# Four small transformer layers in one kernel: MLP up projections as three fp32r passes, pairwise statistics, new step orders

## What is computed

```
L0: x = x + attn(ln1(x), ctx) Wo + b;            x = x + gelu(ln2(x) W1 + b1) W2 + b2     16 heads of 16
L1: a = attn(x, [ctx, x]) Wo + b + x;            x = x + gelu(rms(a) W1 + b1) W2 + b2     16 heads of 16
L2: x = x + attn(ln(x), ctx) Wo + b  (twice);    x = x + gelu(ln(x) W1 + b1) W2 + b2      16 heads of 128, plus a bias key and value
L3: x = x + attn(ln1(x), ln1(x)) Wo + b;  x = x + attn(ln2(x), ctx) Wo + b;  x = x + gelu(ln3(x) W1 + b1) W2 + b2
```

## Time and profile before

| | |
|---|---|
| median of 3 runs | 1079.56 us (1079.14 to 1081.27) |
| profiled execution | 1081.11 us, its span 1079.8 us |
| PE busy | 1045.6 us, 97% |
| DVE, ACT, POOL busy | 706.6, 602.2, 572.0 us |
| granted TensorE clock | 0.998 of 2.4 GHz |
| stages | A to about 305 us, B to about 814 us, C to the end |

### The profile page before, as it was taken

The page is one execution under the profiler, slowest core; times in us unless marked ns, Lnnn a source line. Parts: engine busy times, 40 slices in busy tenths (PEclk is TensorE's granted clock), DMA queues, the critical chain, the costliest instruction groups (busy, mean ns, idle before and its releaser), DMA issues.

```text
span 1079.8 us, 20226 instructions
## 1 busy us (share of the span) xinstructions
PE 1045.6 (97%) x7794; PEld 917.4 (85%) x7794; DVE 706.6 (65%) x1088; ACT 602.2 (56%) x1323; POOL 572.0 (53%) x618
## 2 busy tenths in 40 slices
PE   6899999999999999999999999999999999988999
PEld 5788788788888999999998999999998887866887
DVE  6888778879537556555658655655654377988840
ACT  4998887778653232223334323322226489999972
POOL 7555535455664434333466434443525378999860
PEclk9999999999999999999999999999999999999999
DMA  9200000000113222122120111101100000000000
GB/s 336 112 2 21 2 1 1 2 1 2 49 42 96 70 69 59 40 79 79 40 76 26 40 40 39 40 29 31 31 1 2 1 1 1 2 2 2 10 11 20
DMA packets 33783, 40.66 MB, mean 38 GB/s; under 512 B 2111, under 2 KB 31257, under 8 KB 32025
## 3 DMA queue, kind: packets, MB, share of 16 engines
q1 hardware_dynamic: 33689, 39.38, 11.1%
HBM read 38.32 MB, written 1.05 MB: 36 GB/s over the span
## 4 chain that ended last, share of the span: by engine, by line
PE 77%; POOL 9%; issue 5%; DVE 5%; ACT 4%; DMA 0%; SPq 0%; POOLq 0%; DVEq 0%; ACTq 0%
PE psum L489 14%; PE psum L663 13%; PE psum L557 10%; PE psum L677 7%; PE psum L723 7%; PE psum L583 5%; PE psum L711 5%; PE psum L691 4%; POOL C tile L1371 3%; PE psum L573 3%; PE psum L598 3%; PE psum L700 2%; PE psum L541 2%; PE psum L610 2%; POOL C tile L1377 2%
## 5 line engine op out<-in xcount | busy, mean ns | idle before, releaser
L1459 POOL TENSOR_TENSOR B tile<-B tile,B rec 128x1024 f32<-128x1024 f32 x32 | 60.7, 1897 | 207.8 <-DVE B rec L994 207.8
L1377 POOL TENSOR_TENSOR A tile<-A tile,outer rec 128x1024 f32<-128x1024 f32 x48 | 90.4, 1894 | 99.4 <-DVE outer rec L887 99.4
L1257 ACT ACTIVATE B own<-B max 128x8 f32<-128x8 f32 x32 | 6.7, 210 | 163.1 <-DVE B tile L981 163.1
L1198 ACT ACTIVATE A tile<-A tile,outer min 128x128 f32<-128x128 f32 (+1 forms) x256 | 92.1, 459 | 3.6 <-DVE outer min L880 3.5
L1126 ACT ACTIVATE B kT<-psum,B bcol 128x1024 f32<-128x1024 f32 x32 | 35.6, 1113 | 90.8 <-PE psum L663 90.8
L489 PE MATMUL psum<-A hT,weights 128*128 128x256 f32 x352 | 81.2, 381 | 2.0 <-ACT A hT L1126 2.0
L489 PE MATMUL psum<-C hT,weights 128*128 128x256 f32 x352 | 80.3, 381 | 1.3 <-DVE C tile L870 1.1
L1198 ACT ACTIVATE C tile<-C tile,outer min 128x128 f32<-128x128 f32 x256 | 77.5, 398 | 3.2 <-DVE outer min L880 3.2
L1022 DVE TENSOR_TENSOR x_all<-x_all,psum 128x512 f32<-128x512 f32 x64 | 42.6, 685 | 54.3 <-PE psum L723 54.3
L489 PEld LDWEIGHTS psum<-A hT,weights 128*128 128x128 f32 x352 | 65.2, 190 | 12.5 <-ACT A hT L1126 3.2
L489 PEld LDWEIGHTS psum<-C hT,weights 128*128 128x128 f32 x352 | 65.5, 190 | 11.3 <-issue 2.1
(11 more groups left out here) (197 smaller groups left out, 3113.6 us busy)
## 6 DMA issues: line engine op xcount, KB each, us to landing
weights<-in_weights_c SPq DMA_DIRECT2D x6, 1024.0 KB, 6.9
raw<-in_wq SPq DMA_DIRECT2D x32, 128.0 KB, 2.7
raw<-in_wk SPq DMA_DIRECT2D x32, 128.0 KB, 2.8
raw<-in_wv SPq DMA_DIRECT2D x16, 256.0 KB, 2.7
raw<-in_wo SPq DMA_DIRECT2D x16, 256.0 KB, 2.8
weights<-in_weights_a SPq DMA_DIRECT2D x1, 3072.0 KB, 21.7
weights<-in_weights_a SPq DMA_DIRECT2D x1, 2048.0 KB, 11.3
wide<-in_bias_v SPq DMA_DIRECT2D x2, 1024.0 KB, 10.6
```

The lines of the kernel that those rows point to most:

```text
L1198: i = act.activation(of_head, of_head, ACT.Exp, bias=part.min[:, u % 4, h:h + 1], scale=-1.0)
L1377: pool.tensor_tensor(tile(u, ly.nk), tile(u, ly.nk), part.rec[:, u % 4, 0:ly.per].unsqueeze(2).to_broadcast([P, ly.per, ly.nk]), ALU.mult) ...
L1459: pool.tensor_tensor(tv, tv, m.brec[:, h, :].unsqueeze(2).to_broadcast([P, B, S]), ALU.mult).then_inc(s["normalised"].sem, s["normalised"] ...
```

## The change

What it does:

- **Up projections in three passes.** `up` multiplies as stage B does, 12 fp32r matmuls a step. For this each MLP's up weights are cut by GpSimd in four quarters (`cut_up`, steps `cut L0 0` and so on; for M2 in turns 2 to 4 and 7 of the second round of stage B), and each stream's features into `hi` and `lo`: for L0, M2 and L3c VectorE drains the transposed rows with scale and offset into the space of `xn` (`split`), ScalarE rounds that into `hi` (`upper`), GpSimd subtracts (`lower`). For L1, whose norm has no offset, ScalarE drains straight into `hi` and VectorE subtracts it from the bank.
- **Space.** `lo` of the weights takes the place of the weights, `hi` that of `raw` (L0), of L0's first weights (L1), of used rows of biases and a tile of stage C (M2), and of new tiles (L3c). Stage C has four key and value slots in place of five. The int32 mask has a tile of its own.
- **Statistics** of both batches of a stream in one step: two `bn_stats`, two `bn_aggr`, one addition and one power on 128x2; `xn` is one step a stream too.
- **Loads.** SyncE loads heads 0 and 1 of stage B, which go to `raw`, behind L0's last `up`.
- **Orders.** Both texts are new; they have 413 and 302 steps in place of 437 and 330. Units of L3 run as s0, s1, s2, c0, c1, s3, c2, c3.

The diff, cut to its core:

```diff
-SLOTS = {"L0": (0, 1, 0, 1), "L1": (0, 1, 0, 1), "L3s": (0, 1, 2, 3), "L3c": (NS, 0, 1, 2)}
+SLOTS = {"L0": (0, 1, 0, 1), "L1": (0, 1, 0, 1), "L3s": (0, 1, 2, 0), "L3c": (3, 1, 2, 3)}
...
+        self.w_hi = {"L0": quarters(self.raw_hi), "L1": quarters(self.weights_lo), "M2": [self.rows_hi[:, n * C:(n + 1) * C, :] for n in range(3)] + [m2_hi],
+                     "L3c": l3_hi}
...
-                features(event, part.xn[k], z, "ACT")
+                features(event, part.xn[k], z, "parts" if of == "mlp" else "ACT")
...
         def up(name, k, o, z):
+            event, lo = (name, "up", k, o), lo_signal(name)
             if o == 0:
-                wait_features((name, "mlp", k))
-            if name == "L0":
-                once("w_mlp0_loaded", 16)
-            by_features((name, "up", k, o), "up_projected", "up_drained", m.w[UP[name][0]], part.hT[k], o, z)
+                pe.wait_ge(s[lo].sem, s[lo].at((name, "mlp", k)))
+            pe.wait_ge(s["up_lo_made"].sem, s["up_lo_made"].at((name, o // 2)))
+            claim(z, "up_drained", event)
+            d.take(event, z)
+            w = m.w_hi[name][o // 2], m.w_lo[UP[name][0]][:, :, o * P:(o + 2) * P]
+            h = part.hi[k], part.lo[k]
+            for n in range(2):
+                for c in range(C):
+                    for wp, hp in PASSES:
+                        i = pe.matmul(bank(z)[:, n * T:(n + 1) * T], w[wp][:, c, n * P:(n + 1) * P], h[hp][:, c, :],
+                                      start=(c, wp, hp) == (0, 0, 0), stop=c == C - 1 and wp == 1)
+            i.then_inc(s["up_projected"].sem, s["up_projected"].mark(event))
...
+        def split(name, k):
+
+            event, (scale, offset) = (name, "mlp", k), LN[name, "mlp"]
+            z, scale = d.bank[event], m.col[scale]
+            if offset is None:
+                dve.wait_ge(s["hi_drained"].sem, s["hi_drained"].at(event))
+                for c in range(C):
+                    i = dve.scalar_tensor_tensor(out=part.lo[k][:, c, :], in0=bank(z)[:, c * T:(c + 1) * T], scalar=scale[:, c:c + 1],
+                                                 in1=part.hi[k][:, c, :], op0=ALU.mult, op1=ALU.subtract)
+                i.then_inc(s["lo_drained"].sem, s["lo_drained"].mark(event))
+                return
+            dve.wait_ge(s["turned"].sem, s["turned"].at(event))
+            for c in range(C):
+                i = affine(part.h(k)[:, c, :], bank(z)[:, c * T:(c + 1) * T], scale[:, c:c + 1], m.col[offset][:, c:c + 1])
+            i.then_inc(s["h_drained"].sem, s["h_drained"].mark(event))
...
+        def upper(name, k):
+            event = (name, "mlp", k)
+            act.wait_ge(s["h_drained"].sem, s["h_drained"].at(event))
+            act.copy(part.hi[k][:, :, :], part.h(k)).then_inc(s["hi_drained"].sem, s["hi_drained"].mark(event))
...
+    def cut_up(name, n):
+
+        if name == "L0" and n == 0:
+            pool.wait_ge(s["w_mlp0_loaded"].sem, 16)
+            pool.wait_ge(s["cols_turned"].sem, s["cols_turned"].at("cols"))
+        elif name == "L1" and n == 0:
+            pool.wait_ge(s["w_one_loaded"].sem, 16)
+            pool.wait_ge(s["out_projected"].sem, s["out_projected"].at(("L0", NS - 1, SB - 1)))
+        elif name == "M2" and n == 0:
+            pool.wait_ge(s["w_c_loaded"].sem, 16 * (NP_ - 2))
+        elif name == "L3c" and n == 0:
+            pool.wait_ge(s["weighed"].sem, s["weighed"].at((2, NP_ - 1, 1, 1)))
+        w, of = UP[name][0], slice(n * 2 * P, (n + 1) * 2 * P)
+        pool.tensor_copy(m.w_hi[name][n][:, :, :], m.w[w][:, :, of]).then_inc(s["up_hi_made"].sem, s["up_hi_made"].mark((name, n)))
+        pool.wait_ge(s["up_hi_made"].sem, s["up_hi_made"].at((name, n)))
+        pool.tensor_tensor(m.w_lo[w][:, :, of], m.w[w][:, :, of], m.w_hi[name][n][:, :, :], ALU.subtract).then_inc(
+            s["up_lo_made"].sem, s["up_lo_made"].mark((name, n)))
...
+        def lower(name, k):
+            event = (name, "mlp", k)
+            pool.wait_ge(s["hi_drained"].sem, s["hi_drained"].at(event))
+            pool.tensor_tensor(part.lo[k][:, :, :], part.h(k), part.hi[k][:, :, :], ALU.subtract).then_inc(
+                s["lo_made_h"].sem, s["lo_made_h"].mark(event))
...
             if what == "stats":
-                rstd(tuple(a), part.ve[a[2]][:, a[3]:a[3] + 1], part.rstd[a[2]][:, a[3]:a[3] + 1], 1)
+                rstd(tuple(a), part.ve[a[2]][:, :], part.rstd[a[2]][:, :], SB)
...
         cut_output(j, turn)
+        if j == 2 and 2 <= turn < 5:
+            cut_up("M2", turn - 2)
...
         if turn:
             divide(j, turn, 1)
+        if last and j == 2:
+            pool.wait_ge(s["bv_drained"].sem, s["bv_drained"].at((2, NP_ - 1, 3)))
+            cut_up("M2", 3)
...
-    load_qk(1, 0)
-    sp.wait_ge(s["cols_turned"].sem, s["cols_turned"].at("cols"))
-    load_qk(1, 1)
     sp.wait_ge(s["turned"].sem, s["turned"].at(("ctx", NS - 1)))
     load_bias_v(1)
-    sp.wait_ge(s["mask1_made"].sem, s["mask1_made"].at("mask"))
+    for k in range(NS):
+        sp.wait_ge(s["up_projected"].sem, s["up_projected"].at(("L0", "up", k, FC - 2)))
+    load_qk(1, 0)
+    load_qk(1, 1)
     load_v(1, 0)
     load_o(1, 0)
```

More of the change, by code:

```diff
@@ L430 @@
[L430 to L432 removed]
+    output 0, cut L3c 0, stats M2 mlp 0, xn M2 mlp 0, output 1, output 2, residual M2 mlp 0, stats M2 mlp 2, xn M2 mlp 2, turn_in M2 mlp 0 5, output 3,
@@ L433 @@
+    xn L3c mlp 3, up L3c 2 6 1, turn_in L3c mlp 3 2, down L3c 2 0 3, up L3c 3 0 1, residual L3c mlp 3, up L3c 3 2 2, up L3c 3 4 0, up L3c 3 6 7,
+    down L3c 2 1 0, down L3c 3 0 7, down L3c 3 1 2
 """
@@ L1204, in do @@
             elif what == "turn_in":
-                features(tuple(a[:3]), part.hT[a[2]], LN[a[0], a[1]])
+                if a[1] == "mlp" and a[0] != "L1":
+                    upper(a[0], a[2])
+                else:
+                    features(tuple(a[:3]), (part.hi if a[1] == "mlp" else part.hT)[a[2]], LN[a[0], a[1]])
             elif what == "k":
@@ L1390, in do @@
             elif what == "xn" and tuple(a[:2]) != ("L1", "mlp"):
-                _, _, k, b = a
-                pool.wait_ge(s["rstd_made"].sem, s["rstd_made"].at(tuple(a)))
-                shift(tuple(a), part.mv[k][:, b, 0:1], part.rstd[k], part.nb[k], b)
+                name, of, k = a
+                pool.wait_ge(s["rstd_made"].sem, s["rstd_made"].at((name, of, k)))
+                for b in range(SB):
+                    shift((name, of, k, b), part.mv[k][:, b, 0:1], part.rstd[k], part.nb[k], b)
+            elif what == "turn_in" and a[1] == "mlp" and lo_signal(a[0]) == "lo_made_h":
+                lower(a[0], a[2])
+            elif what == "cut":
+                cut_up(*a)
             elif what == "residual":
```

257 lines of the change are left out of this document (139 added, 118 removed).

## The result

The changed kernel took 1072.84 us (median of 5 runs, 1070.16 to 1073.25), the kernel before 1081.27 (5 runs, 1079.14 to 1083.63): a ratio of 0.9916, with a 95% interval from 0.9897 to 0.9934. Five more runs in a later group gave 1071.39 and a ratio of 0.9917. The profiled execution took 1073.25, its span 1072.0. Forecast were 1065.6, in a range from 1056 to 1074: faster, as said, but by 8.4 us in the first group and 9.5 in the later one, and not by 14.

The account below looks back on a forecast made before the run. TensorE, busy 1045.6 of 1079.8 us, was taken as the bound, except where GpSimd and ScalarE fill late stage C. Savings of 8.7 (A), 0 (B) and 5.3 (C) sum to 14.0: median 1065.6 us, range 1056 to 1074.

Parts of the forecast that it names:

- Part 1: Up projections: 12 passes of 120 ns replace 8 float32 records a step, 18.4 us of TensorE saved, bounds 11 to 22.
- Part 2: Stage A: 9.2 us of TensorE saving comes through, less 0.5 for features; cuts hidden; 8.7 us gained.
- Rival 5: Passes cost the page's 109 ns, so 8.5 us more is removed, about 1057 us; chance 0.02.
- Part 3: Stage B: GpSimd's four cuts of M2's weights stay hidden, 0 us; without cover 2 us lost.
- Hidden, by 0.3 us: Stage B turns with a cut: the division ends 0.65 us later, at 656.5, before TensorE's transposes at 656.82.
- Part 4: Stage C: 9.2 us of TensorE saving less 3.9 for start, M2's last stream and engine load; 5.3 us gained.
- -2.2, at most -4: Stage C's start: paired normalisation and longer features make TensorE wait, 2.2 us lost, at most 4.
- Together -0.5, at most -4: Stage C from 870: GpSimd's lower parts, fewer powers and ScalarE's function switches lose 0.5 us, at most 4.
- Rival 2: Stage C gives nothing, as GpSimd and ScalarE set 870 to 1030; 1070.9 us, to 1074; chance 0.16.
- 900 to 1000 still GpSimd's: Sign that the forecast is right: in stage C's stretch from 900 to 1000 us GpSimd still sets the pace.
- Rival 1: New order also regains 5.8 us from 900 to 1000 and loses nothing at C's start; 1057.6 us; chance 0.19.
- Rival 3: Lower parts reached too early hold GpSimd's queue in the GpSimd-bound stretch; slower, 1090 us; chance 0.07.
- Rival 4: Passes are not cheaper, 144 ns each; within 0.2% or a little worse, 1080 us; chance 0.04.

Follow-up runs that it names:

- e1_a_fp32: Changed kernel with stage A's up projections (L0, L1) as float32 products of the rounded upper parts alone: 1082.3 us, ratio 1.001 to the kernel before.
- e1_c_fp32: Changed kernel with stage C's up projections (M2, L3c) as float32 products of the rounded upper parts alone: 1078.93 us, ratio 0.9981 to the kernel before.
- e6_pair_before: Kernel before, with only the pairing of both batches' statistics and normalisations at the second batch's step: 1087.88 us, ratio 1.0069 to the kernel before.
- e9_unpaired: Changed kernel with each batch's statistics, variance step and power by itself again, at the same step: 1073.59 us, ratio 0.993 to the kernel before.
- e2_c_two: Changed kernel with two of the three passes in stage C's up projections (M2, L3c): 1068.12 us, ratio 0.9876 to the kernel before.
- e7: Changed kernel with three of eight exponentials of each of stage C's 32 tiles left out: 0.3 us less between C's first and last division.
- e8: Changed kernel with stage C's mask step on GpSimd made on four of eight heads: 2.0 us less between C's first and last division.
- e10: Changed kernel with fewer exponentials and the mask on four of eight heads in stage C: first to last division 160.7 us, 8.7 less.
- e4_lower_dve: Changed kernel with the subtraction for stage C's lower features on VectorE at the first up step: 1087.08 us, ratio 1.0055 to the kernel before.

## Why the prediction was right or wrong

**Part 1, the price of a pass: half right.** A run of 48 passes took 5.87 us from its first start to the next instruction's, 122 ns each, and the steady distance is 118. But the first distance in a run of passes is 0.20 to 0.31, 0.22 in the timeline above, and most runs are short: in stage A, 14 of 21 are one step of 12 by itself, at 1.50 to 1.62 us instead of 1.44. All of stage A's 32 steps took 48.4 us with passes and 55.8 in float32 (e1_a_fp32), 0.23 a step and not 0.288. So the groups of `up` give 14 us for 64 steps where I wrote 18.4; the bounds held. I took the price from a long run and applied it to short ones.
The Trainium skill (TensorE: Matmul & The Clock Gate, "Back-to-back issue gap") would give 109 ns by its formula, which it calls one for an isolated gap, without a budget for weight loads. Here every matmul has its weight load, and the steady distance is 118. Rival 5, which took 109, fell with that.

**Part 2, stage A: right, in part by luck.** 8.7 forecast; 7.1 and 9.1 in two executions, 9.6 for the passes alone by experiment, of which only 7.4 stand in `up` itself, where I had 9.2. The rest is time saved at neighbours (0.9 in the transposes of the weights, 0.5 in `project`), for which the sum had no term. The cuts were hidden, as worked out, and GpSimd waited 79 us for reciprocals in A. What was missed is the opening: the first scores come 2.1 us apart in two executions, 1.7 by a clock of 0.79 from 12 to 20 us and 0.4 by a load, which is inside the 3 us allowed for it.

**Part 3, stage B: wrong by 0.5 us, and for a reason that I had not seen.** 0.4 of it lie in the turns with a cut. The turns with a cut take 31.55, 31.53 and 31.53 us instead of 31.40. GpSimd's timeline in the first of them:

```profile
645.59 0.61 POOL L1414 CAST rows hi<-weights 128x512 fp32r<-128x512 f32 x1
646.29 1.29 POOL L1416 TENSOR_TENSOR weights lo<-weights,rows hi 128x512 fp32r<-128x512 f32 x1
647.92 1.90 POOL L1560 TENSOR_TENSOR B tile<-B tile,B rec 128x1024 f32<-128x1024 f32 x1 [0.34 <-DVE B rec L1054]
```

The division still waits 0.34 us for VectorE's reciprocal: the queue of GpSimd did not delay it. VectorE's timeline, in the turn before, without a cut, and in this one:

```profile
615.05 0.17 DVE L1050 SCALAR_TENSOR_TENSOR B sum<-B own,B sum 128x8 f32<-128x8 f32 x1
615.25 0.20 DVE L1054 RECIPROCAL B rec<-B sum 128x8 f32<-128x8 f32 x1
...
646.45 1.15 DVE L1050 SCALAR_TENSOR_TENSOR B sum<-B own,B sum 128x8 f32<-128x8 f32 x1
647.64 0.20 DVE L1054 RECIPROCAL B rec<-B sum 128x8 f32<-128x8 f32 x1
```

A step of 0.17 us takes 1.15 and ends as GpSimd's subtraction ends (647.60 and 647.58): as the shared lock above would have it for an instruction with two SBUF inputs. The division comes 0.99 us later than in the turn before, where I had 0.65, and the 0.97 us of slack in the earlier trace rows are just used up. "Hidden, by 0.3 us" had the right slack and the wrong delay.

**Part 4, stage C: wrong, 5.3 forecast, 1.2 measured.** Of the 4.1 that are missing, 1.7 are the passes' worth, 1.3 the clock and 1.2 what the rest of the change costs.
- The start: "-2.2, at most -4". The first `down` comes 35.1 us after B's last scores, 31.8 before: 3.3 lost, of which 1.3 are the clock, which no step of the prediction had. Without the clock 2.0, and 3.0 with float32 products (e1_c_fp32): that term was small by 0.8 at most, and 2.0 of the 3.0 are regained by the first division. The sentence that the clock "is 1.00 in all these windows" is a right reading of the kernel before, and was carried over to one that waits more there.
- The passes' worth: 9.2 less 1.2 for M2's last stream was to be 8.0; e1_c_fp32 shows 6.3. The groups of `up` give 6.8, 0.21 a step and not 0.288; the middle loses 1.2 of its 2.5 to waits, as the term had it, and 0.7 come from neighbours. So it is Part 1's price again.
- "Together -0.5, at most -4" for GpSimd's and ScalarE's load was too small in the middle. C without the passes is 3.9 longer than before: 1.0 up to the first division, 2.0 in the middle (170.6), 1.0 in the tail. Against 2.2 + 0.5 that is 1.2 too little. I counted engine time gained and lost and found it even. That a step's place counts too is shown by the old order, where the pairs cost 5.8 in C (e6_pair_before). In the new order undoing them gains nothing (e9_unpaired), so which part of the change costs the 3.9 is not shown.

The tail's hand-off was hidden as forecast: its last `up` steps begin at 1053.33 without a wait. So 6.3 - 3.9 - 1.3 = 1.1 for stage C, where 8.0 - 2.7 was forecast; with 7 to 9 from A and 0.5 lost in B these are the 8.4 to 9.5 measured. The total stayed in the range because that was wide enough to hold a stage C that gives almost nothing, not because C's sum was right.

**Rivals.** Rival 2 (C gives nothing, 1070.9 to 1074) is what happened in size, and its mechanism for the middle is in the main what e2_c_two, e7, e8 and e10 show: the middle took 168.6 before and 169.3 after. "Set" is a little too strong, since e1_c_fp32 lengthens the middle by 1.3. It had a chance of 0.16 although show ScalarE at 93.63 and GpSimd at 92.53 of 100: with two engines above 90% beside TensorE it should have been the first reading. The sentence "900 to 1000 still GpSimd's" was wrong in its singular. Rival 1 fell: the order regained nothing net. Rival 3's mechanism did no harm in the change: GpSimd does stand up to 6.4 us for a rounded part at C's start, 4.3 in the tail and 6.5 in A, where it has time, but in C's middle 0.4 us at most. e4_lower_dve shows that it exists, with 15 us, on VectorE. Rival 4 fell with the 118 ns.

What stays open: which part of the change costs the 3.9 us of stage C (order, features' longer way, cuts and lower parts on GpSimd were not taken apart); how the 5.8 us of the pairs in the old order split between the later place and the lock was not traced, and pairs whose variance step stays 128x1 twice, with one power of 128x2, were not tried; nor was the old order with the passes. The clock's fall was prevented by work in the gaps, but not brought about at will.

## What to carry to other kernels

Before a saving on one engine is counted in full, look for the engines beside it in the same stretch: where three are above nine tenths, taking 22 us from ScalarE or 30 from GpSimd shortened the stretch by 0.3 or 2.0 us, and only taking from both at once shortened it by 8.7. Measure what a cut takes by busy time, not by durations added up, since instructions of one engine overlap. Price a step by runs of its own length, not by the steady distance of a long run. Where a change lengthens a wait of TensorE at the start of a stage, look at the granted clock behind it as well as at the wait, and where a step is moved or merged, ask what the queue behind it was doing meanwhile, not only how many instructions it has.

## What the runs showed of the hardware that was not expected

- TensorE's granted clock fell to 0.51 for 3.5 us when it was already at work again: after 7.5 us with 4.13 busy and idle stretches of 1.38, 0.80 and 1.20 us in between, and 0.9 us into an unbroken run of matmuls. With 27 transposes of 128x128 ahead of it and in the gaps it stayed at 1.00. At the low level the passes start 213 ns apart instead of 118.
- A VectorE instruction of 128x2 (or with two SBUF inputs) took up to 1.63 us in stage C of the changed kernel, and up to 1.83 in stage A, instead of 0.17 beside a GpSimd instruction, and ended with it; a variance step of 128x1 with one input never did (56 of 56 in the kernel before).
- In a run of fp32r matmuls of 128x128 by 128x256 the first start to start is 0.20 to 0.31 us and the steady one 0.12.
- Exponentials of 128x128 on ScalarE overlap: 256 of 399 ns each are busy for 77.4 us, 302 ns each.
